# Moving SBUF tensors so that stationary operands start 64 bytes behind moving ones, in a fused feed-forward and attention kernel

## The reference

```
x = x + 0.5 * ffn(layernorm(x))
x = x + attention(layernorm(x))
x = x + 0.5 * ffn(layernorm(x))
ffn(x)  = (silu(x @ w_gate.T) * (x @ w_up.T)) @ w_down.T              # hidden width 1024
attention: rows scaled to unit norm and by gamma, one product with w_qkv
  (16 query heads, 4 key and 4 value heads of 64), rotary embedding of queries and keys,
  causal softmax(q k.T / 8) @ v, then one product with w_out
```

## The kernel before

| tensors | remainder of the start, before |
|---|---|
| gate, up, down, qkv, out weights, hi and lo | 128 |
| `xf_t`, `xa_t`, `q_t`, `k_t`, `v_parts`, `hid_hi`, `hid_lo`, `xn`, `probs`, `q_rot`, `k_rot` | 192 |
| `p_even`, `p_odd`, `o_t` | 128 |
| `eye_sb` | 160 |

## Time and profile before

### The profile page before, as it was taken

The page is one execution under the profiler, slowest core; times in us unless marked ns, Lnnn a source line. Parts: engine busy times, 40 slices in busy tenths (PEclk is TensorE's granted clock), DMA queues, the critical chain, the costliest instruction groups (busy, mean ns, idle before and its releaser), DMA issues.

```text
span 584.4 us, 13692 instructions
## 1 busy us (share of the span) xinstructions
PE 561.9 (96%) x4364; PEld 532.6 (91%) x4364; DVE 432.6 (74%) x1295; ACT 379.5 (65%) x1013; POOL 361.0 (62%) x344
## 2 busy tenths in 40 slices
PE   7788999999999999999999999999999999999997
PEld 3777999999999999999999999999999999789997
DVE  3687987769767795868867697777868698698533
ACT  4445892589736895379925897369934897379422
POOL 0556572887649765695838875597737877445322
PEclk9799999999999999999999999999999999999999
DMA  7340000350006200270004400080003500000001
GB/s 220 117 130 2 2 2 20 90 129 1 20 18 165 50 18 0 60 174 0 18 18 114 101 18 0 18 197 19 18 18 74 141 0 0 18 1 2 2 1 37
DMA packets 28090, 29.70 MB, mean 51 GB/s; under 512 B 2976, under 2 KB 25888, under 8 KB 28064
## 3 DMA queue, kind: packets, MB, share of 16 engines
q1 hardware_dynamic: 28064, 29.37, 19.3%
HBM read 8.39 MB, written 2.10 MB: 18 GB/s over the span
## 4 chain that ended last, share of the span: by engine, by line
PE 69%; DVE 9%; issue 8%; SPq 5%; POOL 4%; ACT 3%; DMA 2%; POOLq 0%; DVEq 0%; ACTq 0%
PE bank L958 44%; PE bank L967 9%; PE bank L1092 5%; PE bank L1062 5%; SPq L292 3%; PE bank L1087 3%; PE bank L1058 2%; SPq L281 2%; PE bank L1054 1%; DVE rope_s L722 1%; POOL probs L404 1%; DVE hid L839 1%; POOL hid_lo L413 1%; DMA eye_sb<-in_eye 1%; ACT xn L483 1%
## 5 line engine op out<-in xcount | busy, mean ns | idle before, releaser
L404 POOL TENSOR_TENSOR probs<-probs,inv_sum 128x512 f32<-128x512 f32 (+1 forms) x64 | 93.9, 1470 | 56.0 <-DVE inv_sum L807 55.9
L547 ACT ACTIVATE probs<-probs,neg_max 128x128 f32<-128x128 f32 (+1 forms) x256 | 113.2, 450 | 4.1 <-DVE neg_max L797 3.9
L413 POOL TENSOR_TENSOR hid_lo<-hid,hid_hi 128x512 fp32r<-128x512 f32 x64 | 83.0, 1301 | 36.2 <-ACT hid_hi L587 35.0
L958 PE MATMUL bank<-xf_t_hi,gate_hi 128*128 128x256 f32 x256 | 75.5, 295 | 7.1 <-DVE gate_lo L650 3.7
L958 PE MATMUL bank<-down_hi,hid_hi 128*128 128x256 f32 x256 | 73.0, 285 | 1.6 <-POOL hid_lo L413 1.6
L958 PE MATMUL bank<-xf_t_hi,up_hi 128*128 128x256 f32 x256 | 72.2, 282 | 0.0
L958 PE MATMUL bank<-xf_t_hi,gate_lo 128*128 128x256 f32 x256 | 71.9, 281 | 0.0
L958 PE MATMUL bank<-xf_t_lo,gate_hi 128*128 128x256 f32 x256 | 71.9, 281 | 0.0
L958 PE MATMUL bank<-down_lo,hid_hi 128*128 128x256 f32 x256 | 71.8, 281 | 0.0
L958 PE MATMUL bank<-down_hi,hid_lo 128*128 128x256 f32 x256 | 71.7, 280 | 0.0
L958 PE MATMUL bank<-xf_t_hi,up_lo 128*128 128x256 f32 x256 | 71.3, 279 | 0.0
(11 more groups left out here) (141 smaller groups left out, 1832.3 us busy)
## 6 DMA issues: line engine op xcount, KB each, us to landing
q_t<-rotated SPq DMA_DIRECT2D x96, 128.0 KB, 2.7
k_t<-rotated_k SPq DMA_DIRECT2D x48, 128.0 KB, 2.7
x_in<-in_x SPq DMA_DIRECT2D x7, 256.0 KB, 2.7
out<-y_out SPq DMA_DIRECT2D x7, 256.0 KB, 2.1
probs<-in_w_qkv SPq DMA_DIRECT2D x4, 384.0 KB, 3.8
probs<-in_w_gate SPq DMA_DIRECT2D x2, 512.0 KB, 7.0
probs<-in_w_up SPq DMA_DIRECT2D x2, 512.0 KB, 7.9
probs<-in_w_down SPq DMA_DIRECT2D x2, 512.0 KB, 4.2
```

Source lines behind the costliest of these rows:

```text
L404: nc.gpsimd.tensor_tensor(part, part, inv_sum[:, slot].unsqueeze(2).broadcast_to([P, GROUP, keys]), ALU.mult).then_inc(p_done, 1)
L413: nc.gpsimd.tensor_tensor(hid_lo[:, slot].rearrange("p c n -> p (c n)"), hid[:, slot], hid_hi[:, slot].rearrange("p c n -> p (c n)").bitca ...
L547: last = nc.scalar.activation(part, part, ACT.Exp, bias=neg_max[:, slot, g:g + 1], scale=-1.0, accum_out=row_sum[:, slot, g:g + 1])
L958: last = nc.tensor.matmul(dst, a[x], b[y], start=start and i == 0, stop=stop and i == 2, skip_group_check=shared)
```

## The change

It changes only the order and the padding of SBUF tensors; no instruction, wait, count or shape changes. A 64-byte pad in front of the weights, a 256-byte one in front of the moving operands and a 128-byte one in front of `hid_hi` set the remainders; `sb` takes an alignment for the pads.

```diff
+ROW = 256
...
-        def sb(name, shape, dt=F32):
-            return ctx.enter_context(nc.sbuf_tensor(name, shape, dt))
+        def sb(name, shape, dt=F32, align=32):
+            return ctx.enter_context(nc.sbuf_tensor(name, shape, dt, align_bytes=align))
...
+        sb("before_weights", [P, ROW // 4 // 4], align=ROW)
         gate_w = [sb(f"gate_{s}", [P, KC, HID], F32R) for s in ("hi", "lo")]
         up_w = [sb(f"up_{s}", [P, KC, HID], F32R) for s in ("hi", "lo")]
         down_w = [sb(f"down_{s}", [P, HID // P, DIM], F32R) for s in ("hi", "lo")]
         qkv_w = [sb(f"qkv_{s}", [P, KC, QKV], F32R) for s in ("hi", "lo")]
         out_w = [sb(f"out_{s}", [P, OC, DIM], F32R) for s in ("hi", "lo")]
+        q_t = sb("q_t", [P, KV_HEADS, GROUP, SEQ], F32R)
+        v_parts = sb("v_parts", [P, 6 * KV_HEADS + 1, DH], F32R)
...
+        neg_max = sb("neg_max", [P, 4, GROUP])
+        row_sum = sb("row_sum", [P, 4, GROUP])
+        inv_sum = sb("inv_sum", [P, 4, GROUP])
+
+        sb("before_moving", [P, ROW // 4], align=ROW)
+        xf_t = [sb(f"xf_t_{s}", [P, KC, SEQ], F32R) for s in ("hi", "lo")]
+        xa_t = [sb(f"xa_t_{s}", [P, KC, SEQ], F32R) for s in ("hi", "lo")]
+        k_t = sb("k_t", [P, KV_HEADS, 2, SEQ], F32R)
+        rope_sb = sb("rope_sb", [P, 2, SEQ])
+        rope_rows = sb("rope_rows", [P, NT, 2, DH // 2])
+        mask_sb = sb("mask_sb", [P, SEQ])
+        eye_sb = sb("eye_sb", [P, P])
+        x_in = sb("x_in", [P, NT, DIM])
...
+        xn = sb("xn", [P, NT, DIM])
         hid = sb("hid", [P, 2, 2 * P * NT])
-        hid_hi = sb("hid_hi", [P, 2, 2, SEQ], F32R)
-        hid_lo = sb("hid_lo", [P, 2, 2, SEQ], F32R)
...
         p_even = [sb(f"p_even_{s}", [P, NT, GROUP * P], F32R) for s in ("hi", "lo")]
         p_t = [p_even, p_odd]
+        sb("before_stationary", [P, ROW // 2 // 4], align=ROW)
+        hid_hi = sb("hid_hi", [P, 2, 2, SEQ], F32R)
+        hid_lo = sb("hid_lo", [P, 2, 2, SEQ], F32R)
         o_t = [sb(f"o_t_{s}", [P, NT, 2, GROUP, P], F32R) for s in ("hi", "lo")]
```

More of the change, by code:

```diff
@@ L125, in build @@
         factor = sb("factor", [P, NT])
-        hid = sb("hid", [P, 2, 2 * P * NT])
-        hid_hi = sb("hid_hi", [P, 2, 2, SEQ], F32R)
-        hid_lo = sb("hid_lo", [P, 2, 2, SEQ], F32R)
-        q_t = sb("q_t", [P, KV_HEADS, GROUP, SEQ], F32R)
-        k_t = sb("k_t", [P, KV_HEADS, 2, SEQ], F32R)
-        v_parts = sb("v_parts", [P, 6 * KV_HEADS + 1, DH], F32R)
+        neg_max = sb("neg_max", [P, 4, GROUP])
[10 more added lines that the diff above has]
+        x_in = sb("x_in", [P, NT, DIM])
+        x1_next = sb("x1_next", [P, NT, DIM])
+        x1 = sb("x1", [P, NT, DIM])
+        x2 = sb("x2", [P, NT, DIM])
+        xn = sb("xn", [P, NT, DIM])
+        hid = sb("hid", [P, 2, 2 * P * NT])
         with nc.sbuf_tensor("rotated", [P, KV_HEADS, 2, 2, SEQ], F32R) as rotated:
@@ L145, in build @@
         o_sums = sb("o_sums", [P, GROUP * P])
-        neg_max = sb("neg_max", [P, 4, GROUP])
-        row_sum = sb("row_sum", [P, 4, GROUP])
-        inv_sum = sb("inv_sum", [P, 4, GROUP])
         with nc.sbuf_tensor("rope_c", [P, 2, 2, SEQ], F32) as rope_c:
```

## The result

The changed kernel takes 583.34 us (median of 5 runs, 583.04 to 584.00), where the kernel before takes 587.93 (585.89 to 590.73, five runs). The ratio is 0.9931, with a 95% interval of 0.9910 to 0.9951. The profiled execution took 584.0 us. In the changed kernel every line number named so far is higher by 3.

The account below looks back on a forecast made before the run. PE's own pace bounds the kernel wherever PE does not wait. Terms 4.4 - 0.6 - 0.6 + 0.8 = 4.0 us took the profiled 586.27 to 582.3; the median stands 1.66 higher, so 583.9 us, range 580.8 to 587.6.

Parts of the forecast that it names:

- stretch B: The part of each turn paced by PE itself, 39.7 us in turn 1; predicted to last 39.1 us.
- The rival that nothing moves: Paces hang on history alone or on rows of another length, so the time stays 587.9 us; chance 0.12.
- Half way: Products at +64 settle as now, short in about half the runs: gain 1.7 us, 586.2 us; chance 0.18.
- Part 1: 256-column products in stretch B go to +64, five in six runs short: gain 0.74 us a turn, 4.4 us in six.
- Part 2: Transposes in stretch B go from +32 to 0, 2.4 ns more for each of 44 steps a turn: 0.6 us lost.
- Part 3: In stretch B one `gate` a turn waits for VectorE and loses what is won ahead of it: 0.6 us lost.
- Part 4: Stretch A, including `qk` at +64 and `value_rows` at -64: no gain, covered by the DMAs.
- stretch A: The part of each turn, 28 us, ended by statistics, normalisation, rotation and 24 DMA issues; PE's pace in it is hidden.
- Part 5: Opening and ending: half of 2.2 us for 736 matmuls outside the loop, less 0.3 us for transposes: 0.8 us gained.
- DMAs that land earlier: Restacking DMAs with sources at 0 instead of 192 shorten stretch A by 2.5 us in all: 581.4 us; chance 0.08.
- The rival on the other side: Transposes at distance 0 make the next products lock at 118 ns: 2.1 us more, 590.0 us; chance 0.08.
- the signs named: Timeline: `projection`, long `scores`, `gate` and `up` behind transposes, `down` behind `projection` at 113 ns; longer wait before last `scores`.

Follow-up runs that it names:

- the repetition: The changed kernel unaltered, run again on the same chip as three other layouts: 582.49 us, ratio 0.9905 to the kernel before.
- the sweep: Six kernels, the changed kernel with other pad lengths, each giving all operand pairs one distance (0, +32, +96, 128, -64, -32): 585.93 to 590.73 us.
- at distance 0: The changed kernel with two pads at other lengths, so that every operand of a product is at remainder 0: 590.73 us, ratio 1.0061.
- the borders at +64: Changed kernel with stationary operands at 64, moving at 0, so +64 also where products meet: 583.66 us; with transposes at +64 too, 582.59 us.

## Why the prediction was right, and where it was not

The forecast was 583.9 us, and the median is 583.34, in the repetition 582.49. The mechanism held: the distance of the operands sets the pace that PE can reach, and stretch B turns every nanosecond of it into time. That the two reads of one row get in each other's way was my picture of it; the runs show that the pace depends on the distance, and not why. That the sum came so close is partly luck, because three of its terms were off and cancel.

- **The rival that nothing moves** is out. It drew on "SBUF — State Buffer" (SBUF: two separate sides) of the Trainium skill, by which PE does not wait for SBUF; the sweep disagrees, with 119.4 against 115.1 ns a step for the same instructions.
- **Half way** (586.2 us) had runs settle as they did before, short in about half, and lost part of the gain. The short share of 63% to 68% lies between its half and the forecast's five in six, but the time lies with the forecast, 2.9 us from this rival.
- **Part 1** (4.4 us, 0.74 a turn) was over-sized: the 256-column matmuls of stretch B take 0.54 us a turn less, 3.2 us in six. I let five in six steps run short (114.6 ns); 63% to 68% did, 115.1 and 114.9 ns. Of the missing 1.2 us, 0.5 ns for some 236 steps a turn are about 0.7. The rest is in the start: I reckoned from 118 ns on average, and the steps of the kernel before average 117.5. The first `up` behind transposes still runs at 118 in six turns of six, though *-64* was the reason that I gave for it.
- **Part 2** (0.6 us lost) did not happen. Transposes at distance 0 take 0.87 us for eight and 0.44 for four, as before. I had taken the opening's `scores` as the price of 128 columns at 0, but these average 111 to 112 ns a step in every layout tried, at +64 too, so the 111.4 ns were no price of the distance.
- **Part 3** (0.6 us lost to tight waits) did not come where I had put it. The `gate` that waits for VectorE still does, but its first step averages 158 ns over the six turns, against 167 before, so nothing was lost there. A second wait turned tight, the values of the last heads: VectorE ends `p_odd_lo` (L710 of the changed kernel) late for them. Turn 3, VectorE, then PE's weight load and PE:

```profile
293.86 0.68 DVE L710 TENSOR_TENSOR p_odd_lo<-bank,p_odd_hi 128x512 fp32r<-128x512 f32 x1
```

```profile
294.65 0.19 PEld L1095 LDWEIGHTS bank<-p_odd_hi,v_parts 128*128 128x128 f32 x1
```

```profile
294.56 0.28 PE L961 MATMUL bank<-down_hi,hid_lo 128*128 128x256 f32 x1
294.67 0.48 PE L1095 MATMUL bank<-p_odd_hi,v_parts 128*128 128x512 f32 x1
294.99 0.39 PE L1095 MATMUL bank<-p_odd_lo,v_parts 128*128 128x512 f32 x1
```

`p_odd_lo` ends at 294.54, and the load that elsewhere starts with the last matmul of `down` (294.56) starts at 294.65. The step from the first to the second values' matmul is 320 ns there, and 231 where nothing is late; over the six turns the mean is 279, against 236 before, so 0.04 us a turn. That is 0.3 us in all where I took 0.6. Too much gain in part 1 (1.2 us) and too much loss in parts 2 and 3 (0.6 and 0.3) nearly cancel, which is why stretch B came out at the 39.1 us that I had named.

- **Part 4** (nothing in stretch A) held for this change: its six stretches sum to 166.9 us against 167.3, and nearly all of the difference is in turn 1 (28.07 against 28.42). But "covered by the DMAs" was true by a small margin only. SyncE's row of DMAs begins 9.9 us into turn 2 before, after and at distance 0, and PE comes to the last `scores` just before they land. The last matmul of `down` and that `scores`, turn 2, before, after, and at distance 0:

```profile
193.91 0.28 PE L958 MATMUL bank<-down_hi,hid_lo 128*128 128x256 f32 x1
194.18 0.50 PE L1058 MATMUL bank<-k_t,q_t 128*128 128x256 f32 x2
```

```profile
194.86 0.28 PE L961 MATMUL bank<-down_hi,hid_lo 128*128 128x256 f32 x1
195.23 0.50 PE L1061 MATMUL bank<-k_t,q_t 128*128 128x256 f32 x2
```

```profile
197.41 0.28 PE L961 MATMUL bank<-down_hi,hid_lo 128*128 128x256 f32 x1
197.53 0.40 PE L1061 MATMUL bank<-k_t,q_t 128*128 128x256 f32 x2
```

  A step is 0.12 us, so PE waits 0.15 us before, 0.25 after and not at all at distance 0. A faster PE gains nothing in A; a slower one loses beyond 0.15 us. At distance 0 stretch A of turn 2 is 28.00 us instead of 27.71.
- **Part 5** (0.8 us): the ending gave 0.6. The opening's share can't be read, because the low clock covers it. The medians fell by 4.6 us and, in the repetition, by 5.2, the loop and the ending by 4.2 in the profiled pair; what is left may be the opening's.
- **DMAs that land earlier**, a rival: they did not shorten A, because SyncE's issuing paces them (9.9 us into the turn, eight rows of 1.2 to 2.6 us, as before).
- **The rival on the other side**, that transposes at 0 spoil the products behind them, gave 590.0 us and did not come. In small, something like it may exist: with the borders at +64, stretch B takes 0.16 us a turn more with the transposes at 0 than at +64, though other tensors differ there too.
- Of the signs named, `projection` and `down` behind it at 113, B at 39.1 and the longer wait ahead of the last `scores` came true. The long `scores` did in part: eight in a row step at 113.3 ns in turns 1, 4 and 6 and at 118 in the others (before at 118 to 120). `value_rows` at -64 did not go to 118; it kept the 113.3 of the `qk` ahead of it. `gate` and `up` behind it went the other way, from 113.3 to 118 in all six turns although their distance is +64 now; in stretch A that costs nothing. `gate` and `up` behind transposes are at 113 in part only.

## What to carry to other kernels

Where PE streams without waits and the pace of equal matmuls differs by place, compare the start addresses of the stationary and the moving operand modulo 256 bytes. Avoid equal remainders above all (119.4 ns a step here against 115.1 at +64); a pad of 64 bytes costs no instruction. The numbers are for float32r matmuls of 256 columns with a weight load each; other shapes and types were not tried, but for the 128-column matmuls, which did not react. Judge it by the time of the whole kernel, since neighbours decide if a run settles at the pace that its distance allows, and count only those stretches in which no transfer or other engine ends the wait.

## What the runs showed of the hardware

- 256-column `float32r` matmuls without waits, at distances of 0 and +-64, step at 113.3, 118 or 120 ns, and a run mostly keeps one of these over dozens of matmuls. At distance 0 nearly all are at 120 (1% short). Of the kernels with one distance for all, only those at +64 have over 25% short (47% to 69%).
- The absolute position does not matter as far as seen: +64 was made of 192 and 128 before, and of 64 and 0 or 128 and 64 after, and each of these reaches 113.3. `o_t` lies at 128 in both kernels; only the out weights moved, from 128 to 64, and the last `projection` went from 120 to 113.3.
- Transposes of 128 columns step at 109 ns at 0, +32 and +64 alike, and the opening's `scores` of 128 columns at 111 to 112 at every distance tried.
- The source remainder of the restacking DMAs shows in the packets' time. The row of the DMA queue in the page, before and after:

```profile
q1 hardware_dynamic: 28064, 29.37, 19.3%
```

```profile
q1 hardware_dynamic: 28064, 29.37, 18.1%
```

  The last figure is the share of 16 engines' span. In the eleven kernels with `rotated` and `probs` at 0 it is 18.0 to 18.3%; in the two with them at 192 and at 64 it is 19.3%, while the target `q_t` stood at seven different remainders without a trend. The median time from issue to landing of `q_t` is 2.6 against 2.7 us. In the loop, the 18432 packets of the restacking alone take 67.8 ns on average before and 67.1 with the source at 64, against 61.3 to 62.2 with it at 0, so that the staging of weights in `probs`, which moved along, is not what makes the difference. "DMA: Bandwidth & Descriptors" (How a descriptor splits into AXI transactions) of the Trainium skill says that a transfer off a 256-byte boundary fetches from the one below. The direction agrees; the size is less than the 38 beats for 32 that the prediction worked out from it (19%), since 67.8 against 61.3 ns is 11%. For this kernel's time it was worth nothing that could be measured.
